# A banded-attention kernel on one core: a third buffer for the split of the scores' operands, a last store in two, and the places of the stages' events set anew

## The reference

```python
x = x + 0.5 * ffn(layernorm(x))     # 8 experts, the best 2 of a token
x = x + attention(layernorm(x))     # 16 heads of 16, |q - k| <= 128, token 0 global
x = x + 0.5 * ffn(layernorm(x))
# in ffn: an expert whose tokens are over its capacity is left out whole
keep = jnp.bincount(a_e, length=E) <= cap     # cap = int(1.25 * 8192 / 8)
valid = keep[a_e]
```

## Time and profile before

| | us |
|---|---|
| median of 3 runs | 853.0 (851.11 to 855.2) |
| the profiled execution, its own time | 860.27 |
| its span, first to last instruction | 858.5 |
| PE busy in it | 813.1 |
| DVE busy in it | 743.9 |
| ACT busy in it | 634.3 |
| granted TensorE clock, mean | 0.994 |

### The profile page before, as it was taken

The page is one execution under the profiler, slowest core; times in us unless marked ns, Lnnn a source line. Parts: engine busy times, 40 slices in busy tenths (PEclk is TensorE's granted clock), DMA queues, the critical chain, the costliest instruction groups (busy, mean ns, idle before and its releaser), DMA issues.

```text
span 858.5 us, 50533 instructions
## 1 busy us (share of the span) xinstructions
PE 813.1 (95%) x21504; PEld 613.5 (71%) x21505; DVE 743.9 (87%) x2788; ACT 634.3 (74%) x1418; POOL 481.7 (56%) x856
## 2 busy tenths in 40 slices
PE   9798999899999999899999999899999999998997
PEld 8555666667788777667778778666777777766674
DVE  7898798898987899998988889998988789998964
ACT  2258977898877666898787766789787766787970
POOL 3212555675554475766554556767556455755871
PEclk9999999999999999999999999999999999999999
DMA  7632124241212335442221335624221333424003
GB/s 230 109 92 66 63 75 129 85 129 62 84 60 82 123 106 161 117 126 79 67 83 62 90 114 148 167 65 121 70 82 61 93 116 95 148 68 125 6 28 105
DMA packets 93194, 83.55 MB, mean 97 GB/s; under 512 B 17568, under 2 KB 92192, under 8 KB 92960
## 3 DMA queue, kind: packets, MB, share of 16 engines
q1 hardware_dynamic: 91360, 78.91, 30.3%
q10 hardware_dynamic: 1600, 1.31, 1.0%
HBM read 20.66 MB, written 8.39 MB: 34 GB/s over the span
## 4 chain that ended last, share of the span: by engine, by line
PE 71%; DVE 10%; ACT 9%; issue 4%; SPq 3%; DMA 2%; POOL 1%; DVEq 0%; ACTq 0%
PE bank L1112 14%; PE bank L1060 12%; PE bank L1094 12%; PE bank L949 10%; PE bank L964 7%; PE bank L932 6%; DVE bank L1507 5%; ACT probs L1236 4%; PE bank L1132 3%; PE bank L916 2%; PE bank L868 2%; SPq L844 2%; DMA q_stack<-pieces 1%; PE bank L883 1%; ACT pieces L1186 1%
## 5 line engine op out<-in xcount | busy, mean ns | idle before, releaser
L1236 ACT ACTIVATE probs<-bank 128x384 f32<-128x384 f32 (+1 forms) x1024 | 459.7, 481 | 143.1 <-PE bank L1094 129.1
L1507 DVE CUSTOM_DVE_ANT_0 bank<-bank,con 128x288 f32<-128x288 f32 x1024 | 495.0, 519 | 56.7 <-PE bank L1060 48.2
L1060 PE MATMUL bank<-k_stack,q_stack 96*32 96x288 bf16 x4096 | 327.6, 289 | 11.3 <-DVE row_max L1507 4.5
L1094 PE MATMUL bank<-q_stack,k_stack 99*32 99x288 bf16 (+4 forms) x4096 | 320.9, 285 | 13.3 <-ACT probs L1236 10.1
L1112 PE MATMUL bank<-probs,v_sb 128*32 128x128 f32 x5888 | 307.6, 273 | 4.0 <-issue 2.6
L1306 POOL TENSOR_SCALAR_AFFINE_SELECT probs<-probs 128x512 f32<-128x512 f32 x240 | 155.1, 646 | 177.3 <-ACT probs L1236 176.8
L1112 PEld LDWEIGHTS bank<-probs,v_sb 128*32 128x32 f32 x5888 | 194.7, 110 | 36.6 <-issue 6.1
L1060 PEld LDWEIGHTS bank<-k_stack,q_stack 96*32 96x32 bf16 x4096 | 127.9, 95 | 72.4 <-DVE row_max L1507 20.1
L1094 PEld LDWEIGHTS bank<-q_stack,k_stack 99*32 99x32 bf16 x4096 | 125.7, 95 | 71.5 <-ACT probs L1236 46.5
L1311 POOL TENSOR_SCALAR_AFFINE_SELECT probs<-probs 128x512 f32<-128x512 f32 x240 | 153.6, 640 | 17.6 <-ACT probs L1236 17.6
L949 PE MATMUL bank<-xnT,wqk_sb 128*32 128x256 f32 x2048 | 159.3, 381 | 0.6 <-DVE neg_max L1529 0.5
(11 more groups left out here) (123 smaller groups left out, 721.8 us busy)
## 6 DMA issues: line engine op xcount, KB each, us to landing
q_stack<-pieces SPq DMA_DIRECT2D x384, 64.0 KB, 2.7
k_stack<-pieces SPq DMA_DIRECT2D x364, 64.0 KB, 2.7
x_ring<-in_x SPq DMA_DIRECT2D x28, 512.0 KB, 4.6
out_x<-x_ring SPq DMA_DIRECT2D x16, 512.0 KB, 4.1
attn<-in_x SPq DMA_DIRECT2D x4, 512.0 KB, 6.4
wback_sb<-in_wback SPq DMA_DIRECT2D x8, 256.0 KB, 5.4
k_stack<-pieces ACTq DMA_DIRECT2D x20, 64.0 KB, 3.7
q_stack<-neg_max SPq DMA_DIRECT2D x48, 16.0 KB, 2.2
```

What stands on the lines that cost most here:

```text
L1060: last = pe.matmul(a_ring[i % len(a_ring)][SP * s:SP * (s + 1), 0:WIN], q_stack[g % 2][0:KROWS, h, q:q + SP], k_stack[g % 2][0:KROWS, h, q ...
L1094: last = pe.matmul(score_bank(i)[SP * s:SP * (s + 1), start:final], k_stack[g % 2][0:SROWS, h, WINDOW + P * j + SP * s:WINDOW + P * j + SP ...
L1236: act.activation(probs[:, j % 4, h, c0:c1], score_bank(i)[:, c0:c1], ACT.Exp, scale=LOGIT_SCALE).then_inc(S["exp_ready"], 1)
L1507: dve.tensor_tensor_reduce(out=a_ring[i % len(a_ring)][:, 0:WIN], in0=a_ring[i % len(a_ring)][:, 0:WIN], in1=mask, scale=1.0, scalar=con[: ...
```

## The change

`pieces` gets a third buffer. `within`, a row of COUNT, gets `counts`' place in memory. The flag loads of PE and DVE become events of their own (FLAG), 6 quarters behind COUNT. The last chunk is stored by two DMAs, one of its first three tiles and one of the last. And the tables that place the stages are new, nearly all of them, mostly by a few quarters.

```diff
+PIECES = 3
...
-        pieces = [sb(f"pieces{i}", [P, 3, 512], BF16) for i in range(2)]
+        pieces = [sb(f"pieces{i}", [P, 3, 512], BF16) for i in range(PIECES)]
...
-        within = sb("within", [1, 2, E])
+        within = counts[0:1, :, :]
...
-        QK_AT = (-43, -28, -10, 5, 25, 43, 52, 68, 83, 102, 117, 133, 149, 165, 178, 198)
-        QK_APART = (2, 2, 2, 2, 2, 2, 1, 3, 1, 1, 1, 1, 1, 1, 2, 2)
-        STACK_LAG = 22
-        VALUES_AT = (36, 47, 56, 61, 70, 80, 88, 93)
-        VALUES_APART = (2, 1, 1, 2, 2, 1, 1, 0)
+        QK_AT = (-43, -26, -10, 11, 25, 41, 54, 68, 83, 102, 118, 134, 150, 163, 178, 197)
+        QK_APART = (2, 2, 2, 2, 2, 2, 1, 3, 1, 1, 1, 1, 2, 2, 2, 1)
+        STACK_LAG = 14
+        VALUES_AT = (34, 49, 55, 61, 70, 78, 91, 89)
+        VALUES_APART = (2, 0, 1, 2, 2, 0, 0, 2)
...
-        LOGITS_LAG = -2
+        LOGITS_LAG = 10
...
-        COUNT_AT = 16
+        COUNT_AT = 17
+        FLAG_AT = (6, 6)
...
+                begin(count + FLAG_AT[0], "FLAG", 0)
+                opening(count + FLAG_AT[1], "FLAG", 1)
...
-            def store(sp, i):
-
-                for t in range(4):
+            def store(sp, i, tiles):
+
+                for t in tiles:
                     sp.wait_ge(*emptied("PROJECT", i, t))
-                sp.dma_start(rows(out, i), x_tiles(i)).then_inc(store_of[i][0], 16)
+                held = slice(tiles[0], tiles[-1] + 1)
+                sp.dma_start(rows(out, i)[:, held, :], x_tiles(i)[:, held, :]).then_inc(store_of[i][0], 16)
...
-                            if i >= 2:
-                                act.wait_ge(stack_sem(i - 2), stacked(i - 2))
+                            if i >= PIECES:
+                                act.wait_ge(stack_sem(i - PIECES), stacked(i - PIECES))
...
-                store(sp, last_chunk)
+                store(sp, last_chunk, range(3))
+                store(sp, last_chunk, range(3, 4))
```

More of the change, by code:

```diff
@@ new lines, in build @@
+        EARLY_AT_OPENING = (-64, -49, -43, -32)
+        XT_AT_OPENING = (-46, -32, -20, 8)
+        QK_AT_OPENING = (-38, -28, 1, 14, 21, 40, 52, 69, 84, 101, 129, 138, 153, 162, 176, 197)
+        OPENING = {'ORDER_HEADS': -56, 'WBACK': -62, 'FOLD': 170, 'K_ONES': 45, 'FILL': 42, 'QK_APART': 1, 'STACK': 8, 'STACKS': 14}
+        LATE_AT = (99, 115, 131, 145)
+        LATE_AT_END = (52, 68, 84, 111)
+        LATE = {'LOAD': -10, 'TURN_ATTN': 2, 'PROJECT': ((7, 8, 10, 11), (13, 13, 14, 14)), 'BASE': -9, 'MOMENTS': (12, 18, 20, 22), 'RSTD': 23, 'STORE': 20}
@@ L401, in left_out @@
+        LATE_END = {'TURN_ATTN': 1, 'PROJECT': ((6, 7, 10, 10), (14, 14, 15, 15)), 'BASE': -10, 'MOMENTS': (12, 16, 21, 26), 'RSTD': 24, 'STORE': 24}
+        LOADS_AT_END = (-36, -5, 25, 100)
+        COUNT_AT = 17
+        FLAG_AT = (6, 6)
+        OUT_AT = (0, 0, 0, 7, 0, -1, 0, 2, 1, 11, 1, 1, 2, 1, 3, 5)
+        OUT = {'TURN': 0, 'ADD': 0, 'RECIP': 0, 'MULT': 1}
+        MAX_AT = {'KEY0': 0, 'TURN_MAX': 1, 'MAX': 2, 'PIECES': 3, 'P0': -4, 'EXP0': 4}
         def left_out(first, nb, phase, b, c):
@@ L752, in await_stores @@
                     laps = [lap for s, lap in store_of.values() if s is S[f"stored{m}"]]
+                    halves = first and store_of[last_chunk][0] is S[f"stored{m}"]
                     if laps:
-                        sp.wait_ge(S[f"stored{m}"], max(laps))
+                        sp.wait_ge(S[f"stored{m}"], max(laps) + 16 * halves)
             def take_left_out():
@@ L857, in run_sync @@
                             if not (first and i == last_chunk):
-                                store(sp, i)
+                                store(sp, i, range(4))
                     if first:
@@ L921, in run_tensor @@
                             i, t, k = n
-                            if first and (i, t, k) == (last_chunk, 0, 0):
-                                load_flag(pe, mybir.EngineType.PE)
                             if k == 0:
@@ L1117, in run_tensor @@
                             last.then_inc(S["pv_done"], 1)
+                        elif kind == "FLAG" and n[0] == 0:
+                            load_flag(pe, mybir.EngineType.PE)
                         elif kind == "COUNT":
@@ L1200, in run_scalar @@
                             act.wait_ge(*emptied("QK", g, c))
-                            act.activation(pieces[i % 2][:, 1, :], rest[:, :], ACT.Copy)\
+                            act.activation(pieces[i % PIECES][:, 1, :], rest[:, :], ACT.Copy)\
                                .then_inc(S["piece2_ready"], 1)
@@ L1390, in run_vector @@
                             last.then_inc(S["route_step"], 1)
+                        elif kind == "FLAG" and n[0] == 1:
+                            load_flag(dve, mybir.EngineType.DVE)
                         elif kind == "COUNT":
@@ L1407, in run_vector @@
                             i, t = n
-                            if first and (i, t) == (last_chunk, 0):
-                                load_flag(dve, mybir.EngineType.DVE)
                             if t == 0:
```

43 lines of the change are left out of this document (16 added, 27 removed).

## The result

The changed kernel takes 858.57 us (median of 13 runs, 854.56 to 861.75) and the one before, timed beside it, 855.2 us: a ratio of 1.004 (95% interval 1.0021 to 1.0059), **3.4 us slower**. The forecast was 3.2 us faster.

What follows compares the result with a forecast made beforehand. No single wait bounds the kernel: PE and DVE take turns, leaving 45 us of small PE holes. Terms -1.6 - 1.2 - 0.2 + 0.3 - 0.5 = -3.2 us from 853.0 give 849.8 us; 8-in-10 range 843.5 to 856.5.

Steps and rivals of the forecast that it cites:

- The third buffer, -1.6 us: PIECE1's one wait for the stack's DMAs, at 136 us, goes: -1.6 us, at least 0, at most 1.64.
- The last store, -1.2 us: At the end, 384 KB go earlier and 128 KB remain behind the last addition: -1.2 us, bounds -1.4 and 0.
- The flag loads, -0.2: PE's and DVE's flag loads at the end move to where the engine waits anyway: -0.2 us, between 0 and -0.4.
- the end's order, +0.3 us: COUNT before OUT_MULT and TURN one PROJECT later hold a `misc` bank longer: +0.3 us, between 0 and +1.0.
- The opening, -0.5 us: First batch, where FIRST comes earlier and QK less dense: -0.5 us.
- The three later batches, 0: Stages placed anew in the body keep PE's work in its stretch: 0 us for these batches.
- Inside a full stretch an order gives nothing: In the body's full stretch the time is PE's work, busy 99.79 of 100 us, so reordering wins nothing.
- as much again that a bad one could open: Bound for the body's new places: a good order could fill 6.0 us of holes a batch, a bad one open as much.
- Holes filled: Rival: the new order fills a quarter of the body's holes in four batches, 6 us more, 843.8 us; chance 0.26.
- The Trainium skill (Trainium Kernel Development and Optimization, Performance Expectations): Rule: weight loads' busy share, 78.14 of 100 us in the full stretch, leaves a fifth open to a better order.
- Lumps of VALUES at the `misc` banks: Rival: PE waits 0.7 us for ACT to empty a bank, three times a batch, 8.4 us, 858.2 us; chance 0.15.
- The third buffer only moves its wait: Rival: A waits for the chunk's own DMAs instead and the last store gains nothing, 852.6 us; chance 0.11.

Runs made afterwards that it cites:

- buffer_only: The kernel before with the third buffer and nothing else (counts and within share memory): ratio 0.9965 to before, 3.0 us faster.
- parts_only: The changed kernel with every table as before, keeping third buffer, flag events and split last store: ratio 0.999 to before, 0.9 us under.
- end_new: The kernel before with third buffer, flag events, split store and five new tables of the end: 0.9963 of before, 3.2 us under; again 0.9964, 3.1 us under.
- one_store: end_new with the last store in one transfer of 512 KB again: ratio 0.9972 to before, 0.7 us over end_new.
- tables_only: The kernel before with all tables of the changed one, two buffers, old flag loads, one last store: ratio 1.0029 to before, 2.5 us over.
- after_two: The changed kernel with two buffers and not three: ratio 1.0043 to before, 3.7 us over.
- opening_new: The kernel before with third buffer, flag events, split store and the seven new tables of the opening: ratio 1.0002 to before, 0.2 us over.
- body_back: The changed kernel with the body's tables as before, opening and end tables still new: ratio 1.0014 to before, 1.2 us over.
- stack10: The changed kernel with the opening's STACK 10 and not 8, two PIECE1 copies ahead of ACT's five DMA issues: ratio 1.0076 to before, 6.5 us over.
- kones46: The changed kernel with K_ONES 46 and not 45, so ACT's fills of k_stack stand one quarter later: ratio 1.0076 to before.
- values_back: The changed kernel with the opening's VALUES and single stages as before, its QK, FIRST, EARLY and XT new: ratio 1.0066 to before, 5.6 us over.

## Why the prediction was wrong

Three stretches, us by the trace (means, single profiles in brackets):

```
places of          buffers   head tiles 4-63                64-191                  192-247
before             2         168.0 (167.7, 168.3)           402.1 (402.4, 401.8)    172.2 (171.9, 172.4)
before             3         164.4 (164.3 to 164.6, five)   401.2 (400.3 to 401.9)  173.3 (172.9 to 173.8)
the change         3         168.0 (168.6, 166.5, 168.8)    403.2 (401.9 to 404.9)  173.8 (174.8, 173.4, 173.2)
the change         2         167.6 (164.7, 170.4)           404.7 (405.2, 404.2)    175.1 (176.2, 174.0)
```

(The second line has the kernels buffer_only, parts_only, end_new twice and one_store; the last has tables_only and after_two.) From the first line to the third the buffer gives 3.6 us in the opening and the new opening takes them back. The body then loses some 2.7 us (1.1 in batches two and three, 1.6 in the last; held against the second line, 2.0 and 0.5). With 0.3 us for the store and 0.3 us against for the end's order this is +2.7 us, for a measured 2.5 to 3.4. That the two agree so well is partly luck. The sum leaves out what stands ahead of head tile 4, which begins at 33.8 to 34.6 us in the changed kernel and at 35.2 and 36.8 us before, and head tiles 248 to 251; and over the whole span the profiles don't show the loss at all, on average 856.2 us in three of the changed kernel and 856.6 in two of before. The loss is that of the medians, the table says where single executions lost. With two buffers the new opening took 164.7 us once and 170.4 once, so it isn't slow in every execution.

**The third buffer, -1.6 us.** Right in sign, too small: -3.0 alone. It was sized by the wait of one profile, a value that was 0.4 us in the next one, while the stretch around it was 3.5 us too long in both. And the term was taken to stand beside the new places, where it is 0 (after_two).

**The last store, -1.2 us.** -0.3 us. Two steps stand in this term. The first is that 384 KB "can be issued at about 852.95", right behind the third addition. In six of the 13 profiles with two stores SyncE came out of its branch too late for that, and the first transfer went 0.8 to 1.0 us behind the third addition. The trace of before hid it: its branch began at 849.55 and the instruction behind it at 852.89, just when the third addition ended. But this step didn't cost the term. In the other seven the first transfer went 0.2 to 0.3 us behind the third addition, and from the last addition to the end they took 4.3 us on average, the six 4.2. The step that failed is the size of the second transfer, 128 KB "a little over" the 2.7 us of 64 KB: it landed 2.9 to 3.6 us behind its issue, the single 512 KB 3.2 to 3.9 us, and SyncE's record of the second issue is 0.55 to 1.9 us long where that of a single one is 0.37 us. The estimate by the Trainium skill (DMA: Bandwidth & Descriptors, Anatomy of one DMA) of 0.9 us for the bytes was closer and still three times too high.

**The flag loads, -0.2, and the end's order, +0.3 us.** The second as forecast: 6.85 us against 6.59 and 6.44 from the last PV to the first PROJECT of the last chunk, though by the body's tables. The first is below what the runs tell.

**The opening, -0.5 us.** This is one of the two steps that decided. I costed PE's work by quarter and took "FIRST comes earlier and QK less dense" for a gain. PE idled for 7.3 us in head tiles 4 to 39 with the old opening, in every profile within 0.1 us, and for 9.5 to 10.4 us in the three of the changed kernel. What I left out is how long ACT is held by what isn't an exponential: the fourth run of five DMA issues, 3.2 us with the old opening and 4.5 to 4.9 now, and fills of 2.12 us. QK of a chunk moved a few quarters towards them, and PIECE1, REST and the row maximum behind it were late. The traces place this at head tiles 4 to 7, which took 1.3 to 2.2 us more than with the old opening. It isn't the whole: opening_new and body_back have issues of 4.5 us too, with pauses of PE of only 0.9 and 0.7 us near 43 us, and took 168.2 and 169.6 us for head tiles 4 to 63.

A second cost of the opening is the clock. In the seven profiles with the old opening the granted clock was 1.00 from 31 to 150 us. In seven of the eleven with the new opening's tables, or most of them, it fell to 0.50 between 79 and 88 us, for 3.4 us or 6.8, each time behind a pause of PE of 1.3 to 1.7 us for an exponential. A pause of 1.31 us at this place is in the traces of before too, and there the clock stayed. In the third profile of the changed kernel it fell also behind the pause of 1.71 us near 43 us; head tiles 8 to 11 took 10.25 us there and 8.66 in the first. The same stretch in the third profile and in the first:

```profile
45.60:48.90 3.30, 3.30 (x44) 1.69 (x44) 2.42 (x11) 0.40 (x1) 0.43 (x1) 0.50 0.24 73
45.60:48.90 3.30, 3.27 (x72) 1.50 (x64) 3.30 (x16) 0.99 (x2) 1.05 (x2) 1.00 0.24 71
```

**The three later batches, 0.** This is the other. "Inside a full stretch an order gives nothing" was right of the stretch at its best: for each group of four head tiles from 64 to 247 take the shortest time in any profile, and their sum is 570.6 us over nine profiles with the old body and 571.1 over nine with the new. But the sums of the medians are 573.3 and 576.1. Eight of the 46 groups scatter by over 0.5 us with the old places, 16 with the new. (The openings differ within both sets, so part of the scatter may be theirs.) The new order has the same work and, as I read this, less slack: a transfer that lands a microsecond late stops it. The plainest case is the load near 733 us: DVE waited 0.8 to 2.5 us for it in five of the eight profiles with the change's place of the load, and at most 0.26 us in the nine with the old place. The prediction's bound, "as much again that a bad one could open", had the size; the likeliest value didn't ask which wait would end last if a transfer was late.

**The rivals.** Holes filled: no. The Trainium skill (Trainium Kernel Development and Optimization, Performance Expectations) is no help either way here: weight loads were busy for 77.27 of 100 us in the full stretch, before for 78.14, and in all 18 profiles for 75.5 to 78.1, with PE busy for 98.1 to 99.8; no order tried gained anything there. Lumps of VALUES at the `misc` banks: the signature was there in the opening (2.2 us and 1.4 at the longest, from 1.1 and 0.7), the forecast of 858.2 us is near the measured time by accident, since the body has none of it. The third buffer only moves its wait: under the new places its gain is gone, but no wait for the chunk's own DMAs took its place.

**What stays open.** How the loss splits between places in the opening: putting back one table or moving one number made it worse each time (stack10, kones46, values_back). And what PE's pauses without a wait are. Behind 100 us the 18 profiles have 45 of over 0.7 us inside a run of matmuls, 17 with the old body and 28 with the new, and 23 more at the start of a run, the one near 733 us among them. 36 of the 45 have a SyncE issue of 0.9 us or more (0.59 is the usual) within 0.5 us; at a random place some 25 would, so this says less than it seems. The traces say more by counting. Take PE's instructions (matmuls, weight loads, waits) in the order of their starts: every one of these pauses, and every other one of 0.3 us or more, stands before number 193 or 194 (counted from 0) of a block of 256, in all 18 profiles. The one near 733 us stands before the same matmul in eight profiles, 0.7 to 1.1 us in three with the old body and 0.8 to 2.2 us in five with the new. So the place is fixed by the count of PE's instructions, and only its length differs: pauses from 0.3 us up add up to 2.7 to 6.8 us a profile with the old body (mean 4.5) and to 4.3 to 11.9 with the new (mean 7.3). What PE is given once in 256 instructions, and why it is sometimes late, no run here shows.

## What to carry to other kernels

Before sizing a term by one wait in one profile, take a second profile of the same kernel and lay the two side by side, stretch by stretch: what differs may not be there to be won, and what agrees is exact to hundredths. When a hand-placed order is moved, follow the slowest neighbours on each in-order engine (DMA issues on ACT, a fill, a load behind a store), and ask at each place how late a transfer may be before the engine stops; two orders that are equal at their best can be 3 us apart on average. A buffer and a new order that cure the same wait are worth it once, not twice: the buffer alone, with the old places, is 3.0 us faster than before and 6 us faster than the whole change.

## What was unexpected of the hardware

- Behind a pause of PE of 2.20 us the granted clock was 0.50 for 734 to 737 us, behind one of 1.80 us at the same place 1.00. Near 80 us it fell behind pauses of 1.3 us in some profiles and not in others.
- Five DMA issues on ACT took 3.2 us with the old opening and, in eight of nine profiles that have them at the new place, 4.5 to 4.9 us (3.8 in the ninth).
- SyncE needed 3.9 to 4.1 us from a branch to its next instruction in eight of 18 profiles.
- PE paused for up to 2.2 us with nothing that it waited for, always at the same place of a block of 256 of its instructions.
